# Thirteen bias rows loaded once and spread over the partitions by TensorE, and one weight load moved behind the first table blocks

## The reference

```python
xn = _layernorm(x, axis=-1)
x = x + _L0_gnn_ref(xn, edge_index, edge_attr_8, ...) + _L0_mix_ref(xn[None], ...)[0]
```

```python
q = jnp.einsum('blc,chd->blhd', x, Wq) + bq
k = jnp.einsum('blc,chd->blhd', x, Wk) + bk
v = jnp.einsum('blc,chd->blhd', x, Wv) + bv
attn = _favor_bidirectional(q, k, v)
attended = jnp.einsum('blhd,hdc->blc', attn, Wo) + bo
h = _layernorm(attended + x, ln1_scale, ln1_bias)
ff = jax.nn.relu(h @ W1 + b1) @ W2 + b2
return _layernorm(ff + h, ln2_scale, ln2_bias)
```

## Time and profile before

| | |
|---|---|
| median of 3 runs | 2567.64 us (2566.18 to 2568.13) |
| profiled execution, its own time | 2563.54 us |
| its span on the core | 2561.7 us |
| mean granted TensorE clock | 0.93 |
| busy: PE, DVE, ACT, POOL | 87%, 53%, 28%, 31% of the span |
| DMA | 180.62 MB, mean 71 GB/s |

### The profile page before, as it was taken

One profiled execution on the slowest core, in us unless ns is written; L12 is line 12 of the kernel. 1 busy time (PEld: TensorE's weight loads), 2 busy tenths in 40 slices (PEclk: granted clock), 3 DMA queues, 4 the chain that ended last, 5 costly groups with the idle time before them and its releaser, 6 DMA issues.

```text
span 2561.7 us, 31158 instructions
## 1 busy us (share of the span) xinstructions
PE 2222.7 (87%) x11374; PEld 1274.3 (50%) x11374; DVE 1346.4 (53%) x4100; ACT 709.9 (28%) x1573; POOL 798.7 (31%) x552
## 2 busy tenths in 40 slices
PE   1999984998965999997899989988999989898974
PEld 0455552443322444445663457667876653455543
DVE  5455676778963666662114264431122242279996
ACT  3111121221003444442121155653211120133442
POOL 2018888887875565660000000000000000012222
PEclk9998887998987999998999979998899999999987
DMA  9982222222236666653001020001100022000000
GB/s 362 419 339 3 3 3 19 4 4 20 3 35 149 179 171 169 171 142 146 1 1 49 1 107 1 1 1 76 58 1 1 1 58 78 0 1 9 9 9 17
DMA packets 90266, 180.62 MB, mean 71 GB/s; under 512 B 65109, under 2 KB 66070, under 8 KB 74135
## 3 DMA queue, kind: packets, MB, share of 16 engines
q1 hardware_dynamic: 44367, 176.77, 21.3%
q0 software_dynamic: 45072, 1.46, 5.4%
q10 hardware_dynamic: 674, 0.39, 0.1%
HBM read 110.27 MB, written 68.31 MB: 70 GB/s over the span
## 4 chain that ended last, share of the span: by engine, by line
PE 59%; DVE 18%; POOL 10%; ACT 5%; issue 5%; DMA 3%; SPq 0%; DVEq 0%; ACTq 0%; POOLq 0%
PE banks L192 16%; POOL edge_table L506 8%; PE banks L2002 6%; PE banks L2029 5%; PE banks L1435 3%; PE banks L1258 3%; PE banks L1271 2%; DMA edge_table<-arena 2%; PE banks L1813 2%; PE banks L1840 2%; PE banks L1827 2%; PE banks L328 2%; PE banks L186 2%; POOL arena L1215 2%; PE banks L1862 2%
## 5 line engine op out<-in xcount | busy, mean ns | idle before, releaser
L192 PE MATMUL banks<-arena 128*125 128x512 f32 (+1 forms) x1280 | 582.9, 604 | 38.7 <-ACT arena L2531 29.1
L506 POOL DMA_INDIRECT edge_table<-arena x313 | 491.9, 1572 | 249.2 <-DMA edge_table<-arena 158.6
L192 PEld LDWEIGHTS banks<-arena 128*125 128x125 f32 x1280 | 239.3, 195 | 320.6 <-issue 270.5
L1183 DVE TENSOR_TENSOR arena<-banks,arena 125x500 f32<-125x500 f32 x200 | 208.5, 1051 | 162.5 <-ACT banks L1235 158.8
L1215 POOL TENSOR_TENSOR arena<-arena 125x500 f32<-125x500 f32 x180 | 222.6, 1247 | 149.4 <-DVE arena L1183 143.5
L1258 PE MATMUL banks<-arena 64*125 64x250 f32 x800 | 142.6, 434 | 64.8 <-DVE arena L1183 58.2
L2342 POOL MEMSET arena<- 128x1024 f32 x2 | 1.8, 951 | 581.6 <-DVEq L143 581.6
L1950 DVE SCALAR_TENSOR_TENSOR arena<-banks,arena 125x512 f32<-125x512 f32 x80 | 60.1, 751 | 203.7 <-PE banks L2029 203.7
L1235 ACT ACTIVATE banks<-banks 125x500 f32<-125x500 f32 x200 | 114.6, 573 | 173.1 <-PE banks L1261 172.7
L186 PE MATMUL banks<-arena 125*128 125x125 f32 x560 | 92.0, 302 | 69.9 <-DVE arena L180 50.3
L2002 PEld LDWEIGHTS banks<-arena 128*128 128x128 f32 x1280 | 145.7, 194 | 6.9 <-issue 6.8
(11 more groups left out here) (324 smaller groups left out, 3481.2 us busy)
## 6 DMA issues: line engine op xcount, KB each, us to landing
edge_table<-arena SPq DMA_DIRECT2D x24, 2250.0 KB, 36.2
arena<-edge_table SPq DMA_DIRECT2D x50, 984.4 KB
arena<-L_ffn_W SPq DMA_DIRECT2D x4, 2048.0 KB, 8.1
arena<-edge_table SPq DMA_DIRECT2D x50, 114.3 KB
adjacency<-arena SPq DMA_DIRECT2D x50, 109.4 KB
arena<-adjacency SPq DMA_DIRECT2D x10, 546.9 KB
edge_table<-arena POOLq DMA_INDIRECT x313, 3.0
arena<-x SPq DMA_DIRECT2D x1, 2240.0 KB
```

Source lines behind the costliest of these rows:

```text
L192: last = nc.tensor.matmul(dst, xT[:, i, :], w[:, i, 0:n], start=(i == 0), stop=(i == k - 1))
L506: pool.indirect_dma_start(d["table"], bass.IndirectOffsetOnAxis(ap=cell[0:EP, c:c + 1].bitcast(U32), axis=0), vals[0:EP, c * ROW:(c + 1) * ...
L1183: nc.vector.tensor_tensor(P_g[n % PRING][0:TP, :].rearrange("p (e n) -> p e n", e=2), two_scores(n), ring[(c * TILES + b) % RING][0:TP, :, ...
```

## The change

Part one: the thirteen vectors are laid out on the host as one array `L0_bias_rows` with 26 rows of 256 values (row 2i and 2i + 1 are the halves of vector i). One transfer puts it on 26 partitions (`bias_rows`), ahead of `edge_attr_8` in SP's queue. PE spreads vector i with two matmuls whose stationary operand is one column of the identity, repeated 125 times (`spread_bias`), into a PSUM bank, and ACT copies the bank to where the row stood before (`copy_bias`). The nine rows of mix are spread in the edges stage, the four of gnn at the start of the gnn stage. The thirteen broadcasting transfers are gone.

Part two: the load of gnn's `W1` stands behind the loads of the first three table blocks, and so behind the wait for the filled table.

```diff
+        def bias_bank(i):
+            return bank(BIAS_BANKS[i % 4] if i < MIX_BIASES else 2 + i - MIX_BIASES)
+        def spread_bias(pe, i):
+            if 4 <= i < MIX_BIASES:
+                pe.wait_ge(s_bias_out, i - 3)
+            for half in range(2):
+                r = 2 * i + half
+                last = nc.tensor.matmul(bias_bank(i)[0:TP, half * C // 2:(half + 1) * C // 2],
+                                        ident[0:2 * BIASES, r:r + 1].to_broadcast([2 * BIASES, TP]), bias_rows,
+                                        start=True, stop=True)
+            last.then_inc(s_bias_in, 1)
+        def copy_bias(act, i, row):
+            act.wait_ge(s_bias_in, i + 1)
+            nc.scalar.activation(row[0:TP, :], bias_bank(i)[0:TP, :], ACT.Copy).then_inc(s_bias_out, 1)
...
             sp.dma_start(dst_i[0:EP, :].bitcast(I32), d["dst"]).then_inc(s_sd_in, 16)
+            sp.dma_start(bias_rows, d["L0_bias_rows"]).then_inc(s_sd_in, 16)
...
-            for b, n in ((bq_m, "bq"), (bk_m, "bk"), (bv_m, "bv")):
-                load(sp, b, "L0_mix_" + n, s_wm)
...
-            dve.wait_ge(s_sd_in, 32)
+            dve.wait_ge(s_sd_in, 48)
...
             for h in range(2):
                 load_line(act, h)
+            for i, row in enumerate((bq_m, bk_m, bv_m, bo_m, ln1_s, ln1_b, b2_m, ln2_s, ln2_b)):
+                copy_bias(act, i, row)
             for w in (1, 2):
                 act.wait_ge(s_part, 2 * w)
...
+            pe.wait_ge(s_sd_in, 48)
+            for i in range(MIX_BIASES):
+                spread_bias(pe, i)
             for h in range(2):
                 spread_line(pe, h)
...
-            for b, n in ((bo_m, "bo"), (ln1_s, "ln1_scale"), (ln1_b, "ln1_bias"), (b2_m, "b2"),
-                         (ln2_s, "ln2_scale"), (ln2_b, "ln2_bias"), (b1_m, "b1")):
-                load(sp, b, "L0_mix_" + n, s_wm2)
+            load(sp, b1_m, "L0_mix_b1", s_wm2)
...
             sp.wait_ge(s_stage, 3)
-            for b, n in ((bq_g, "bq"), (bk_g, "bk"), (bv_g, "bv"), (bo_g, "bo"),
-                         (lg_g[:, 0:KC], "ln_att_g"), (lg_g[:, KC:2 * KC], "ln_att_b")):
+            for b, n in ((lg_g[:, 0:KC], "ln_att_g"), (lg_g[:, KC:2 * KC], "ln_att_b")):
...
             turned(0)
+            for i, row in enumerate((bq_g, bk_g, bv_g, bo_g)):
+                copy_bias(act, MIX_BIASES + i, row)
...
             turn(0)
+            for i in range(MIX_BIASES, BIASES):
+                spread_bias(pe, i)
+            pe.wait_ge(s_bias_out, BIASES)
             for t in range(TILES):
                 pe.wait_ge(z_cols, t + 1)
...
             sp.wait_ge(s_stage, 6)
-            sp.dma_start(w1_most, d["L0_gnn_W1"][:, 0:3 * HID]).then_inc(s_wf, 16)
-            sp.dma_start(w1_last, d["L0_gnn_W1"][:, 3 * HID:4 * HID]).then_inc(s_wf, 16)
             table_filled(sp)
...
             for i in range(RING):
                 load_block(i)
+            sp.dma_start(w1_most, d["L0_gnn_W1"][:, 0:3 * HID]).then_inc(s_wf, 16)
+            sp.dma_start(w1_last, d["L0_gnn_W1"][:, 3 * HID:4 * HID]).then_inc(s_wf, 16)
```

More of the change, by code:

```diff
@@ L259, in gps_two_layers @@
         s_scat = [sem(f"columns_scattered_{v}") for v in range(2)]
+        MIX_BIASES, BIASES = 9, 13
+        BIAS_BANKS = (3, 5, 6, 7)
+        s_bias_in = sem("bias_rows_spread")
+        s_bias_out = sem("bias_rows_copied")
+        def bias_bank(i):
[12 more added lines that the diff above has]
+            nc.scalar.activation(row[0:TP, :], bias_bank(i)[0:TP, :], ACT.Copy).then_inc(s_bias_out, 1)
         def const_pool(pool):
@@ L531, in gps_two_layers @@
         rd_m = space.take(8)
+        bias_rows = space.take(C // 2)[0:2 * BIASES, :]
         f1_m = [chunks(k_m[:, 2 * TP * v:2 * TP * (v + 1)], TP, 2) for v in range(2)]
@@ L575, in mix_dve @@
             settle(dve, 0)
-            dve.wait_ge(s_wm, 16 * 6)
+            dve.wait_ge(s_bias_out, MIX_BIASES)
             for t in range(TILES):
@@ L610, in mix_dve @@
             link(dve, nc.vector.tensor_copy(kept_rstd[0:TP, :], rstd[0:TP, :]))
-            dve.wait_ge(s_wm2, 16 * 10)
+            dve.wait_ge(s_wm2, 16 * 4)
             def attention_row(t):
@@ L734, in mix_pe @@
         def mix_pe(pe):
-            pe.wait_ge(s_wm, 16 * 6)
+            pe.wait_ge(s_wm, 16 * 3)
+            pe.wait_ge(s_bias_out, MIX_BIASES)
             def after(t):
@@ L772, in mix_pe @@
             pe.wait_ge(m_qT, TILES)
-            pe.wait_ge(s_wm2, 16 * 10)
+            pe.wait_ge(s_wm2, 16 * 4)
             def num_den(t):
@@ L916, in gnn_dve @@
             z(1)
-            dve.wait_ge(s_bg, 16 * 6)
+            dve.wait_ge(s_bias_out, BIASES)
             for t in range(TILES):
@@ L961, in gnn_act @@
         def gnn_act(act):
-            act.wait_ge(s_bg, 16 * 6)
+            act.wait_ge(s_bg, 16 * 2)
             def turned(t):
@@ L2746, in lay_out @@
         o["L0_gnn_" + n] = w4(a["L0_gnn_" + n].T)
-    for n in ("bq", "bk", "bv", "bo", "b2"):
-        o["L0_gnn_" + n] = row(a["L0_gnn_" + n])
+    o["L0_gnn_b2"] = row(a["L0_gnn_b2"])
     for n in ("ln_att_g", "ln_att_b", "ln_ff_g", "ln_ff_b", "b1"):
@@ L2755, in lay_out @@
         o["L0_mix_" + n] = w4(w.reshape(w.shape[0], -1))
-    for n in ("bq", "bk", "bv", "bo", "ln1_scale", "ln1_bias", "b2", "ln2_scale", "ln2_bias"):
-        o["L0_mix_" + n] = row(a["L0_mix_" + n])
+    mix_rows = [a["L0_mix_" + n] for n in ("bq", "bk", "bv", "bo", "ln1_scale", "ln1_bias", "b2", "ln2_scale", "ln2_bias")]
+    graph_rows = [a["L0_gnn_" + n] for n in ("bq", "bk", "bv", "bo")]
+    o["L0_bias_rows"] = np.ascontiguousarray(np.concatenate([v.reshape(2, -1) for v in mix_rows + graph_rows]))
     o["L0_mix_b1"] = col(a["L0_mix_b1"])
```

## The result

The changed kernel took 2556.45 us (median of 7 runs, 2552.96 to 2560.76), the kernel before 2567.64 us in the same sitting: a ratio of 0.9960, 95% interval 0.9948 to 0.9971, so it is faster by 7.4 to 13.4 us. Forecast were 2556.7 us. The profiled execution took 2555.48 us, with a span of 2553.7 us.

A forecast was written before the change was run, and what follows sets the result against it. POOL's chain of 313 scatters was taken to set the time up to about 788 us; -1.4 - 2.7 - 2.2 - 4.6 = -10.9 us there gave 2556.7 us from 2567.64, range 2551.5 to 2562.5.

The forecast's parts named there:

- the chain through DVE and PE: Rival: the profile's chain is right and the turns release scatter 152, so no change, 2565.8 us; chance 0.08.
- Item 1: Zeroing of the table: three broadcasting loads ahead of the zeros go, a 27 KB load comes; -1.4 us, bounds 0 and -1.9.
- Item 2: Scatters 0 to 5: less loss in proportion to the traffic without six bias rows; -2.7 us, bounds 0 and -4.5.
- Items 3 and 4: On POOL: start of gnn without four broadcasting loads, -2.2 us; near 750 us no late scatter beside W1's load, -4.6 us.
- Item 5: Turns, which scatters need settled: +3.8 us at the edges, -1.0 at gnn by middle values; no cost to the time.
- The slack of 2.0 us: What was left of 11.1 us between turn 19 and scatter 152, so that POOL would not wait there.
- The rival with the turns: Both bursts of spreads at the lower clock make scatter 152 wait for turn 19; 2.2 us given back, 2558.9 us; chance 0.13.
- Item 6: W1 loaded behind attention's first three blocks: block 3 still arrives in time, 814 against 815.40 us, at no cost.
- The sum: The four savings on POOL's chain (zeroing, first scatters, start of gnn, W1) together: -10.9 us.

The follow-up runs named there:

- f2: The kernel before, with twelve unneeded scalings (5.8 us) added on ACT at gnn's first tile: 2564.25 us, ratio 0.9984.
- e1: The changed kernel with W1's load back in its old place, so only the bias rows change: 2560.70 us, ratio 0.9977.
- e4: The changed kernel unedited, measured once more: 2559.77 us, ratio 0.9966.
- f3: The changed kernel with twelve unneeded scalings added on ACT at gnn's first tile: 2559.16 us, ratio 0.9961.
- e2: The kernel before with only W1's load moved behind the first three blocks: 2564.72 us, ratio 0.9986.
- g3: The changed kernel with the matrix of bias rows padded by zeros from 26 to 128 rows: 2553.32 us, ratio 0.9948.
- f4: The changed kernel with f1's split and the remaining mix and gnn weights in 40 pieces, each issued after another scatter landed: 2551.21 us, ratio 0.9932.
- e3: The changed kernel with W1 loaded only behind the 21st stored block of attention: 2557.76 us, ratio 0.9956.
- f1: The changed kernel with five of mix's nine copies behind ACT's second bf16 part, the ninth spread behind PE's first key line: 2552.18 us, ratio 0.9944.
- g4: f4 measured once more, unedited: 2553.61 us, ratio 0.9957.
- g1: f4 with gnn's four rows spread at the end of mix: 2550.61 us, ratio 0.9942.

## Why the prediction was right, and where it was not

**What bounds the kernel** held in the profiles. Up to the last scatter POOL sets the time, and f2 shows that the chain through DVE and PE was no path. That a microsecond on POOL's chain is one in the median is not shown: e1 waited 5.2 us there for a late landing and was 0.9 us over e4 in the median; f3 waited 14.8 us, and its median lies between the changed kernel's two.

**Item 1, zeroing**: -1.4 forecast; scatter 0 came 1.7 us earlier in the changed kernel and in e1. That is close by luck. Scatter 0 comes at 168.4, 170.0 and 172.3 us in the three profiles with the broadcasting loads (before, e2, f2) and at 165.8 to 167.5, mean 166.7, in the ten with the load of 27 KB (169.1 in g3, with the larger one). By the means item 1 is -3.5 us, beyond its bound of -1.9; what the three loads cost beyond their bytes, no run separates.

**Item 2, first scatters**: -2.7 forecast, -4.8 measured, and -4.7 to -5.3 in every kernel with the biases and plain loads. The direction was right and the size was not: "in proportion to the traffic" failed, and even the bound of -4.5 was passed. The runs show no law in its place. While the weights come as whole loads the first five scatters lose 10.1 to 10.7 us beside the broadcasting loads and 5.4 to 6.0 without them; with pieces they lose only 0.5 to 0.7. But the same bytes in pieces cost the next 39 scatters most of what they spared the first five (f4). How the loss grows with the bytes, these points don't tell.

**Items 3 and 4** came as forecast on POOL's chain, -2.2 and -4.6; e1 and e2 separate the second there, but not in the median.

**Item 5, the turns**. At the edges +3.8 was taken and turn 0 came 2.0 us later: the spreads were at the dear end of their bounds, but edge_attr_8 was not late, and four copies were done sooner than assumed. At gnn the failed step is "PE is warmed up by then, so the projection takes 3.7": the spreads stayed at the lower level and so did the projection (6.11 us), +1.2 where -1.0 stood. The slack of 2.0 us ("only just") was 1.2.

**The rival with the turns** had 0.13, and that was too little. Of seven profiles with the spreads at gnn, unpadded and undelayed (changed, e1, e3, e4, f1, f4, g4), five show the wait, of 1.2 to 10.9 us; of the four whose code is the changed kernel's up to there (changed, e1, e3, e4), two. I had compared one profile's turn 19 with one profile's scatter 152. But turn 18 was settled anywhere between 405.3 and 416.7 us, and these two ends (e1 and f3) have the same code up to there: a spread of 11 us around a slack of 2. How much of such a wait reaches the end isn't settled: with early spreads the median was 3.0 us lower (g1 against g4, intervals overlapping), while f3's 14.8 us did not show.

**Item 6** is right. No block was late, and e3, with W1 out of the way, is 2.0 us under e4 within overlapping intervals. The rule of the Trainium skill (DMA: Bandwidth & Descriptors, Queues, rings and completion order) that was cited against the move costs nothing here: W1's larger piece took 18.0 us to land, and block 3's sums started at 800.79 us without a wait.

**The sum**: -10.9 forecast, -11.2 measured in the first comparison and -7.2 in the second. It is closer than its terms, and the hit to 0.3 us is luck. In the profiles POOL's chain gained 2.4 us more in items 1 and 2 and 3.3 us that no item has, and the clock behind the table took 8.3 us, which come and go without the change: the short attention stage of e4, the long one of e2, and the last tile's 32.3 us in f3, whose code behind the table is the changed kernel's. The forecast took everything behind the last scatter as rigid; for one profile that does not hold, and for the median it is open (see f3).

## What to carry to other kernels

Ask of a short-lived DMA (here a scatter) what large loads run beside it. Taking bytes away, or moving a load behind the whole run of such DMAs, paid here; cutting the same bytes into pieces mostly spread the delay (against f1 4.8 to 4.9 us less over the first five scatters, but 0.3 to 1.5 us less over the first forty-four). Follow such a saving to the end of the chain, and not only over the stretch where it was made. When a saving on one chain eats the slack of another, compare the slack with the spread of both chains over several executions, not with one profile. Put small PE work where PE has just been busy and nobody waits, not at the start of a stage behind an idle time: the same four spreads cost 4.2 us at the end of mix, where nobody waited, and 7.2 us at the start of gnn, with the first projection behind them.

## What the runs showed of the hardware

Spreads of 26 rows kept PE at work for 7.2 and 8.9 us back to back, and they stayed at the lower level in the ten profiles with them in the edges stage (by their durations) and the eight with them at the start of gnn (granted clock 0.50 in the changed kernel); with 128 rows the clock rose within both bursts. The Trainium skill (TensorE: Matmul & The Clock Gate, Part 1: The HAM clock gate) gives the idle time before a burst as what lowers the clock, and the traces agree (24 us idle ahead of gnn). That it was the number of rows, and not something that came with it, rests on the one profile of g3.

The windows of the changed kernel have a clock of 1.00 from 14 to 37 us, while a spread took 1.7 to 1.8 us there, as at 0.50 around 430 us. The first change that its trace records is a rise at 70.7 us; until then the durations tell the level, not that column.

The same code placed its low-clock stretches differently from execution to execution: attention took 380.3 to 390.1 us, the last tile 32.2 or 35.9, for instance 390.0 and 383.2 us in the changed kernel's two profiles. Its two medians are 3.3 us apart.
